# A two-layer graph network on one core: one fp32 product as three one-pass products, and row scales moved past the matmuls

## The reference

```python
def hypergraph_conv(x, adj, W, b):
    H = (adj != 0).astype(x.dtype)
    w = adj.reshape(N, -1)[:, :C]                  # the first row of adj
    xw = jnp.einsum('ncd,hd->nch', x, W)
    Dn = jnp.einsum('nce,ne->nc', H, w)            # 1/Dn where Dn > 0
    Be = H.sum(axis=1)                             # 1/Be where Be > 0
    m = Be[:, :, None] * jnp.einsum('nce,nch->neh', H, xw)
    out = Dn[:, :, None] * jnp.einsum('nce,neh->nch', H, m)
    return out + b
# layer 0
h = relu(hypergraph_conv(x, adj, W1, b1))          # 512 wide
h = layer_norm(h, gamma, beta)
y = hypergraph_conv(h, adj, W2, b2) + x            # 256 wide
x = _layernorm(x + y)
# layer 1
agg = einsum('bij,bjf->bif', adj, x) / maximum(adj.sum(-1), 1e-6)
x = _layernorm(x + relu(einsum('bnf,of->bno', concatenate([x, agg], 2), WL)))
```

## Time and profile before

| | |
|---|---|
| median of three runs | 1110.2 us (1109.57 to 1110.42) |
| profiled execution | 1110.66 us, span 1108.6 us |
| TensorE busy | 1093.2 us (99%), 6112 matmul records |
| VectorE busy | 699.6 us (63%) |
| ScalarE busy | 314.9 us (28%) |
| GpSimd busy | 182.5 us (16%) |

### The profile page before, as it was taken

How to read it: one execution, slowest core, us unless ns; L and a number is a source line. 1 busy time by engine, 2 the same in 40 slices (tenths; PEclk the granted TensorE clock), 3 DMA queues, 4 the chain that set the end, 5 groups by cost and what they waited for, 6 DMA issues and landing times.

```text
span 1108.6 us, 18544 instructions
## 1 busy us (share of the span) xinstructions
PE 1093.2 (99%) x6112; PEld 899.0 (81%) x6112; DVE 699.6 (63%) x1846; ACT 314.9 (28%) x705; POOL 182.5 (16%) x256
## 2 busy tenths in 40 slices
PE   7999999999999999999999999999999999999997
PEld 6879697796978969688796887969789697887966
DVE  4665595665955768548685486754766646856326
ACT  4342302422124221333113331143301433024220
POOL 0222004120031202211031110401104020041000
PEclk9999999999999999999999999999999999999999
DMA  7017612067211572124611445115442075300001
GB/s 280 20 39 153 150 41 58 0 151 152 55 40 31 120 151 57 38 65 101 146 47 38 96 102 121 41 38 129 103 89 71 4 151 115 65 9 1 1 1 39
DMA packets 64599, 86.18 MB, mean 78 GB/s; under 512 B 9024, under 2 KB 54720, under 8 KB 64576
## 3 DMA queue, kind: packets, MB, share of 16 engines
q1 hardware_dynamic: 63520, 85.88, 33.6%
q10 hardware_dynamic: 1056, 0.00, 0.1%
HBM read 77.47 MB, written 8.39 MB: 77 GB/s over the span
## 4 chain that ended last, share of the span: by engine, by line
PE 94%; DVE 4%; DMA 1%; ACT 0%; issue 0%; ACTq 0%; DVEq 0%
PE bank L731 40%; PE bank L802 10%; PE bank L840 10%; PE bank L862 10%; PE bank L824 10%; PE bank L759 10%; PE bank L832 3%; PE bank L848 1%; DVE adjT L539 1%; DMA small<-in_L_gnn_gamma_dram 1%; DVE HT L544 1%; PE bank L768 1%; DVE o_f L676 0%; DVE xres L680 0%; ACT m_hi L389 0%
## 5 line engine op out<-in xcount | busy, mean ns | idle before, releaser
L731 PE MATMUL bank<-yv,adjT 128*128 128x257 f32 x1024 | 223.3, 380 | 0.0
L731 PEld LDWEIGHTS bank<-yv,adjT 128*128 128x128 f32 x1024 | 194.1, 190 | 31.3 <-issue 3.8
L394 ACT ACTIVATE small<-mv,small 128x1 f32<-128x1 f32 x192 | 56.6, 295 | 362.6 <-DVE mv L521 266.9
L759 PE MATMUL bank<-x_hi,H 128*128 128x258 f32 x512 | 122.8, 289 | 0.8 <-DVE m_lo L526 0.8
L731 PE MATMUL bank<-x_hi,H 128*128 128x256 f32 x512 | 122.6, 283 | 0.0
L731 PE MATMUL bank<-m_hi,HT 128*128 128x256 f32 x512 | 121.6, 281 | 0.0
L731 PE MATMUL bank<-x_lo,H 128*128 128x256 f32 x512 | 121.1, 281 | 0.0
L731 PE MATMUL bank<-m_lo,HT 128*128 128x256 f32 x512 | 120.9, 280 | 0.0
L526 DVE SCALAR_TENSOR_TENSOR m_lo<-bank,small,m_hi 128x256 fp32r<-128x256 f32 x128 | 61.1, 483 | 94.2 <-ACT m_hi L389 94.1
L824 PE MATMUL bank<-W1T,zT 128*128 128x512 f32 x256 | 120.4, 593 | 0.0
L840 PE MATMUL bank<-gW2T,xnT 128*128 128x256 f32 x512 | 119.8, 380 | 0.0
(11 more groups left out here) (80 smaller groups left out, 1621.7 us busy)
## 6 DMA issues: line engine op xcount, KB each, us to landing
raw<-in_adj_dram SPq DMA_DIRECT2D x112, 256.0 KB, 8.5
adjB<-in_adj_dram SPq DMA_DIRECT2D x224, 128.0 KB, 3.4
x_in<-in_x_dram SPq DMA_DIRECT2D x28, 256.0 KB, 4.5
out_dram<-xres SPq DMA_DIRECT2D x112, 64.0 KB, 1.6
raw<-in_adj_dram SPq DMA_DIRECT2D x4, 1024.0 KB, 12.9
w_row<-in_adj_dram SPq DMA_DIRECT2D x8, 512.0 KB, 3.7
x_in<-in_x_dram SPq DMA_DIRECT2D x1, 1024.0 KB, 7.1
out_dram<-xres SPq DMA_DIRECT2D x4, 256.0 KB, 2.2
```

What stands on the lines that cost most here:

```text
L394: nc.scalar.activation(std[:, i:i + 1], mv[:, which, i, 1:2], ACT.Sqrt, bias=eps_c)\
L731: last = mm(bank(stage, i)[:, 0:n_cols], lhsT, rhs, start=(k == 0 and part == 0), stop=(k == NT - 1 and part == parts - 1))
L759: last = mm(*args, start=(c == 0 and n == 0), stop=(c == NT - 1 and n == 1))
```

## The change

P's operands are split in parts of 12 bits, `z` = z_high + z_low and W1 = W1_high + W1_low, whose products are exact in one pass. With high and low scaled copies the sum is made of three products: high x high and low x low go to P's bank, and the cross product of `z_high - 4096 z_low` and `W1_high - 4096 W1_low` to a bank of its own, **M**. The bias row of a tile becomes `hbias` = M x rDn_cross + b1: ScalarE reads M out of PSUM, GpSimd adds b1, and VectorE's hrow adds it to P x rDn_main. The names in the diff are W1_TURN and others for turns of the transpose banks, `SPLIT` = 4096, and `n_side` = 6 for the number of S1 tiles that run step by step.

W2 and WL have the mean of each row taken away once. Then Q of the relu'd row itself, scaled by `rstd_h` as it leaves PSUM, and V of `xres`, scaled by `rstd_1`, need no centring ahead of the transposes. `xres` is still normalised for the residual, now on ScalarE during L. The lags become 1 and 2, there are two slots of `hrow` in place of four, `xnT` lies where `w_row` does, and W2's preparation stands at the sixth step of the first S1.

```diff
-SECOND_CHUNK = {0: (0, 1, 2), 1: (3, 4), 2: (5, 6), 3: (7,)}
-LAG_T = 3
-LAG_Q = 4
-H_SLOTS = 4
+SECOND_CHUNK = {0: (0, 1, 2, 3, 4), 1: (5, 6, 7)}
+LAG_T = 1
+LAG_Q = 2
+H_SLOTS = 2
...
# SyncE
-            sp.dma_start(W2n[:, :, :], W2.rearrange("(t p) d -> p t d", p=P)).then_inc(W2_loaded, 16)
+            sp.dma_start(W1n[:, :, :], W1.rearrange("(t p) d -> p t d", p=P)).then_inc(W1_loaded, 16)
+            sp.dma_start(WLn[:, :, :], WL.rearrange("(t p) d -> p t d", p=P)).then_inc(WL_loaded, 16)
             sp.dma_start(x_in[:, :, :], x[0, :, :].rearrange("(t p) d -> p t d", p=P)).then_inc(x_loaded, 16)
             load_first_rows(0)
...
-                    sp.wait_ge(dn_ready, b * NT + NT)
-                    load_w(b + 1)
...
-                    load_graph(b + 1)
+                    load_raw(b + 1, 0)
+                    load_w(b + 1)
+                    for j in range(1, NT // 2):
+                        load_raw(b + 1, j)
...
# GpSimd
-            pool.wait_ge(rDn_ready, 1)
+            pool.wait_ge(rDn_ready, 2)
...
-                for i in range(NT):
-                    pool.wait_ge(q_hi_done, b * NT + i + 1)
-                    nc.gpsimd.tensor_tensor(x_lo[:, i, :], q_f32[:, i % 2, :], x_hi[:, i, 0:D].bitcast(F32),
-                                            ALU.subtract).then_inc(q_split, 1)
+                for s in range(NT + LAG_Q):
+                    if s < NT:
+                        pool.wait_ge(*emptied("M", s, b))
+                        nc.gpsimd.tensor_tensor(hbias[:, s % 2, :], hbias[:, s % 2, :], b1_row[:, :], ALU.add)\
+                          .then_inc(hbias_done, 1)
+                    if s >= LAG_Q:
+                        i = s - LAG_Q
+                        pool.wait_ge(q_hi_done, b * NT + i + 1)
+                        nc.gpsimd.tensor_tensor(x_lo[:, i, :], q_f32[:, i % 2, :], x_hi[:, i, 0:D].bitcast(F32),
+                                                ALU.subtract).then_inc(q_split, 1)
...
# ScalarE, first graph
-            for e in range(2, NT):
+            for e in range(2, TRANSPOSE_BANKS[0]):
                 take_m_hi("S1", e, 0, e)
+            take_weights(W2_TURN, [gW2T[:, 2 * k:2 * k + 2, :].rearrange("p k o -> p (k o)") for k in range(NH // 2)])
+            act.wait_ge(bank_full[TRANSPOSE_BANKS[0]], BW2_TURN + 1)
+            nc.scalar.activation(bW2_row[:, :], banks[TRANSPOSE_BANKS[0]][:, 0:D], ACT.Copy)\
+              .then_inc(bank_empty[TRANSPOSE_BANKS[0]], 1)
+            for e in range(TRANSPOSE_BANKS[0], NT):
+                take_m_hi("S1", e, 0, e)
...
# ScalarE, each graph
+                take_z_high(0)
+                act.wait_ge(rDn_ready, b * 2 + 2)
                 for s in range(NT + LAG_Q):
+                    if s == max(SECOND_CHUNK):
+                        take_z_high(1)
                     if s < NT:
-                        act.wait_ge(*emptied("P", s, b))
-                        nc.scalar.activation(hrow[:, s % H_SLOTS, :], hrow[:, s % H_SLOTS, :], ACT.Relu)\
-                          .then_inc(relu_done, 1)
-                    if s == max(SECOND_CHUNK) - 1:
-                        take_zT(1)
+                        act.wait_ge(*full("M", s, b))
+                        empties_bank(nc.scalar.activation(hbias[:, s % 2, :], bank("M", s)[:, :], ACT.Identity,
+                                                          scale=rDn_cross[:, s:s + 1]), "M", s)
                     if 0 <= s - LAG_T < NT:
                         i = s - LAG_T
                         act.wait_ge(*full("TH", i, b))
                         empties_bank(nc.scalar.activation(xnT[:, i % 2, :, :].rearrange("p k c -> p (k c)"),
                                                           bank("TH", i)[:, :], ACT.Copy), "TH", i)
                     if s < NT:
+                        act.wait_ge(*emptied("P", s, b))
+                        nc.scalar.activation(hrow[:, s % H_SLOTS, :], hrow[:, s % H_SLOTS, :], ACT.Relu)\
+                          .then_inc(relu_done, 1)
                         root("h", 0, std_h, s, b)
...
+                act.wait_ge(neg_mean_done, b + 1)
+                for i in range(NT):
+                    nc.scalar.activation(xres[:, i, :], xres[:, i, :], ACT.Identity, scale=rstd_1[:, i:i + 1],
+                                         bias=neg_mean_1[:, i:i + 1]).then_inc(normed["1"], 1)
...
# VectorE, each graph
+                take_z_low(0)
+                take_z_cross(0)
                 for s in range(NT + LAG_Q):
+                    if s == max(SECOND_CHUNK):
+                        take_z_low(1)
                     if s < NT:
                         dve.wait_ge(*full("P", s, b))
+                        dve.wait_ge(hbias_done, b * NT + s + 1)
                         empties_bank(nc.vector.scalar_tensor_tensor(
-                            out=hrow[:, s % H_SLOTS, :], in0=bank("P", s)[:, :], scalar=rDn[:, s:s + 1],
-                            in1=b1_row[:, :], op0=ALU.mult, op1=ALU.add), "P", s)
+                            out=hrow[:, s % H_SLOTS, :], in0=bank("P", s)[:, :], scalar=rDn_main[:, s:s + 1],
+                            in1=hbias[:, s % 2, :], op0=ALU.mult, op1=ALU.add), "P", s)
+                    if s == max(SECOND_CHUNK):
+                        take_z_cross(1)
                     if 0 <= s - 1 < NT:
                         inverse_root("h", std_h, rstd_h, s - 1, b)
-                        centre("h", 0, hrow[:, (s - 1) % H_SLOTS, :], rstd_h, s - 1, b)
...
-                        empties_bank(nc.vector.tensor_tensor(q_f32[:, i % 2, :], bank("Q", i)[:, 0:D],
-                                                             bW2_row[:, :], ALU.add), "Q", i)
+                        dve.wait_ge(rstd_done["h"], b * NT + i + 1)
+                        empties_bank(nc.vector.scalar_tensor_tensor(
+                            out=q_f32[:, i % 2, :], in0=bank("Q", i)[:, 0:D], scalar=rstd_h[:, i:i + 1],
+                            in1=bW2_row[:, :], op0=ALU.mult, op1=ALU.add), "Q", i)
...
# TensorE, each graph
+                        pe.wait_ge(*free("M", s, b))
+                        if s == 0:
+                            pe.wait_ge(W1_cross_done, ND)
+                        if s % (CH // P) == 0:
+                            pe.wait_ge(z_cross_done, b * (NCH * ND) + (s // (CH // P) + 1) * ND)
+                        nodes = slice(s * P, (s + 1) * P)
+                        for d in range(ND):
+                            last = mm(bank("M", s)[:, :], z_cross[:, d, nodes], W1_cross[:, d, :],
+                                      start=(d == 0), stop=(d == ND - 1))
+                        fills_bank(last, "M", s)
                         pe.wait_ge(*free("P", s, b))
                         for d in range(ND):
-                            last = mm(bank("P", s)[:, :], zT[:, d, s * P:(s + 1) * P], W1T[:, d, :],
-                                      start=(d == 0), stop=(d == ND - 1))
+                            mm(bank("P", s)[:, :], z_high[:, d, nodes], W1_high[:, d, :], start=(d == 0), stop=False)
+                            last = mm(bank("P", s)[:, :], z_low[:, d, nodes], W1_low[:, d, :],
+                                      start=False, stop=(d == ND - 1))
```

More of the change, by code:

```diff
@@ L92, in graph_net @@
         if s < NT:
+            add_job("M", s)
             add_job("P", s)
@@ L493, in sum_Dn @@
                     dve.wait_ge(dn_ready, b * NT + c)
-                nc.vector.scalar_tensor_tensor(out=unread[:, :], in0=raw[:, c, :], scalar=0.0, in1=w_row[:, :],
+                nc.vector.scalar_tensor_tensor(out=into[:, :], in0=raw[:, c, :], scalar=0.0, in1=w_row[:, :],
                                                op0=ALU.not_equal, op1=ALU.mult,
@@ L518, in moments @@
             def moments(norm, which, src, i, b):
-                nc.vector.bn_stats(stats[:, which, i, :], src)
+                nc.vector.bn_stats(stats[:, i, :], src)
                 dve.drain()
-                nc.vector.bn_aggr(mv[:, which, i, :], stats[:, which, i, :]).then_inc(var_done[norm], 1)
+                nc.vector.bn_aggr(mv[:, which, i, :], stats[:, i, :]).then_inc(var_done[norm], 1)
             def take_m_lo(stage, e, b, n):
@@ L555, in scale_W2T, with centre_weights @@
-            def scale_W2T():
-                for n in range(NH // 2):
-                    dve.wait_ge(bank_empty[TRANSPOSE_BANKS[n]], W2_TURN + 1)
-                    for k in (2 * n, 2 * n + 1):
-                        nc.vector.tensor_scalar(gW2T[:, k, :], W2T[:, k, :], gamma_c[:, k:k + 1], None, ALU.mult)\
-                          .then_inc(W2T_scaled, 1)
+            def centre_weights(parts, done):
+                for n, part in enumerate(parts):
+                    nc.vector.bn_stats(stats[:, n, :], part)
+                dve.drain()
+                for n, part in enumerate(parts):
+                    nc.vector.bn_aggr(mv[:, 0, n, :], stats[:, n, :])
+                dve.drain()
+                for n, part in enumerate(parts):
```

(23 more changed lines are left out.)

229 lines of the change are left out of this document (133 added, 96 removed), and 13 rows, old and new, of the table PRODUCT_BANKS.

## The result

The changed kernel takes 1236.3 us (median of four runs, 1235.1 to 1241.0) against 1109.9 us beside it (1109.2 to 1110.4): a ratio of 1.115 with a 95% interval of 1.112 to 1.118. The profiled execution has a span of 1234.0 us where the one before had 1108.6.

What follows compares the result with a forecast made beforehand. TensorE, busy 99%, bounds the kernel before; after the change a chain of handoffs at 5.50 us a tile does. 1110.66 + 107.2 for eight graphs + 16.4 for the first graph = 1234 us, stated range 1205 to 1280.

Steps and rivals of the forecast that it cites:

- TensorE, P 1.72 to 1.40: P on TensorE: four records become six one-pass products, 0.32 us less a tile, 20.5 us over 64 tiles if TensorE binds.
- The loop, 5.50 us a tile: P stage, relu to relu through moments, q, x_hi, x_lo, add and hrow: 5.50 us a tile against TensorE's 3.57.
- the ring: P stage's handoff chain: hbias(s+1) cannot start until root(s) and x_hi(s-2) are done on ScalarE, so tiles no longer overlap.
- The add, 1.35 between 1.15 and 1.79: GpSimd's 512-column add of b1, shown by no row: taken as 1.35 us, twice x_lo's price, with some start cost paid once.
- One graph, +13.4: From the end of S2's first half to the last Q: 52.0 us against 38.6, 107 us for eight graphs.
- hidden, with 0.6 to spare: Splitting z, some 4.1 us on ScalarE and VectorE, fits beside TensorE's five k-steps (4.7) before M(0); uncovered it costs 4.1.
- Centring and loads, 0: Centring moved into the weights costs nothing; w_row's later load counts 0, between 0 and 3 us a graph.
- rival 3: w_row late as well: VectorE's row sums wait in S3 and m_lo goes late, up to 3 us a graph, 1258; chance 0.07.
- The first graph, +16.4: First graph's setup: +6.3 for a later start and +10.1 for hbias(0)'s add behind GpSimd's residual passes, once, between 6 and 24.
- The sum: Whole kernel: 1110.66 + 107.2 + 16.4 = 1234 us; the main case alone 1212 to 1268.
- Rival 1: TensorE still binds, faster: ScalarE's copy of M runs a tile ahead and TensorE's 3.57 sets the pace, 1106.6; chance 0.05.
- Rival 2: TensorE falls to its lower clock in the gaps: 7.1 us a tile, some 10.6 us a graph more, 1319; chance 0.08.

Runs made afterwards that it cites:

- experiment 11: experiment 9 plus earlier first-graph setup, ScalarE scaling z_low behind relu(1) and doubling the first graph's x: 1104.8 us, ratio 0.9949 against the kernel before.
- experiments 1 to 3: Changed kernel with ScalarE's copy of M a tile ahead, with GpSimd's add ahead of x_lo, then with both: 1224.4, 1231.7 and 1134.2 us.
- 4: Changed kernel with GpSimd's add covering 256 of 512 columns, half of the bias left out: 1199.9 us.
- experiment 7: Changed kernel with VectorE making hbias in one pass from M's bank, without ScalarE's copy and GpSimd's add: 1130.5 us.
- experiment 5: Changed kernel with GpSimd's 16 first-graph residual passes waiting for the bias product instead of the row sums' end: 1234.6 us.
- experiment 3: Changed kernel with both orders changed: ScalarE's copy of M a tile ahead and GpSimd's add ahead of x_lo: 1134.2 us.
- experiment 9: experiment 7 with hbias(s+1) right behind hrow(s), M(s+1) behind P(s), and the second half's z_cross made by ScalarE and GpSimd: 1118.2 us.

## Why the prediction was right

It said 1234 (1205 to 1280) and slower with 0.94; 1236 was measured. The mechanism is the one that it named. That the total fits to 2 us is luck in part: a graph's 13.4 was 1.2 too long, eight times, and against it stood the first graph's 3.4, 1.5 in the second graph and 1.4 of low clock in each of four graphs, none of which is in the sum. By its steps:

- *TensorE, P 1.72 to 1.40.* Right: products 0.23 apart. TensorE would have gained, as experiment 11 shows.
- *The loop, 5.50 us a tile.* Right in its order, link by link, and a little too long: the last five steps have a mean of 5.36. relu to moments 0.66 (predicted 0.66), moments to q 0.87 (0.95), q to x_hi 0.52 (0.52), to x_lo 0.49 (0.49), to the add 0.60 (0.69), to hrow 1.33 (1.40), to relu 0.79 (0.79). What each run showed apart: experiments 1 to 3 that the two orders close the ring, 4 that the add lies on it, 7 that it is gone with the two handoffs.
- *The add, 1.35 between 1.15 and 1.79.* 1.284. The Trainium skill (GPSIMD Engine Reference, Elementwise, side-by-side), from which I had worked out an estimate of 1.25, was nearer here than my doubling of x_lo. The prediction's 0.717 for 256 columns was not "VectorE quiet": from 53.78 to 59.52 VectorE ran hrow, moments and a centring pass of 1.17 instead of 0.55 us. Beside an idle VectorE such a pass took 0.69 in the changed kernel. That page's advice to keep elementwise adds on VectorE (Engine selection) agrees with experiment 7's 741 ns for scale and add in one.
- *One graph, +13.4.* +12.2 from the fourth graph on; 15.2, 13.6 and 13.7 in the three ahead. In the later graphs relu(0) stands 8.2 after the end of S2's first half, as predicted. In the second graph it stood 9.7 after it since M(0) waited 1.16 us for z_cross, with relu(7) at 47.4 (47.2). So "hidden, with 0.6 to spare" failed there: VectorE came late to it.

```profile
219.44 1.29 DVE L688 TENSOR_TENSOR z_low<-bank,z_high 128x512 fp32r<-128x512 f32 x2 [4.60 <-issue]
```

VectorE's idle time there has no releaser. It stands at the first pass through the loop over graphs, and the later graphs don't have it; what it is the runs do not settle.

The other 1.4 us lie behind TH(7), which waits 3.05 us for relu(7) in every graph. In the first three graphs and the last the two Q's after it ran in part at the 1.2 GHz level, in the four between at full speed. The third and the fifth graph, TH(7) and the first product of S3, and the windows over them:

```profile
412.29 1.09 PE L939 MATMUL bank<-ident,hrow 128*128 128x128 f32 x4 [3.05 <-ACT hrow L489]
417.62 0.47 PE L829 MATMUL bank<-x_hi,H 128*128 128x256 f32 x1
...
707.28 0.63 PE L939 MATMUL bank<-ident,hrow 128*128 128x128 f32 x4 [3.05 <-ACT hrow L489]
711.25 0.47 PE L829 MATMUL bank<-x_hi,H 128*128 128x256 f32 x1
```

```profile
411.90:418.00 6.10, 5.71 (x22) 5.01 (x23) 1.89 (x5) 1.86 (x5) 1.34 (x2) 0.72 0.00 0
706.90:713.00 6.10, 5.72 (x34) 5.02 (x35) 2.37 (x6) 2.27 (x6) 1.71 (x3) 1.00 0.05 10
```

From TH(7) to S3 it is 5.33 us in the one and 3.97 in the other.

- *Centring and loads, 0.* Right: VectorE's waits for `w_row` are 1.1 us in all, and rival 3 is out.
- *The first graph, +16.4.* Too small by 3.5: relu(0) at 75.35 instead of 71.9. The residual passes began at 62.28 (59.3 predicted) and took 11.0 us instead of the 10.3 of the earlier trace rows; ahead of them TensorE had waited 3.0 us for H(7), 1.6 for the banks of W2's transposes and 2.8 for their copies. Their share as a cause was over-stated: experiment 5 won 2.7 of the 10.1, 4 at the most, since the row sums and z's split are next.
- *The sum.* The first relu came 3.4 late, all behind it took 102.8 us more than before where the sum had 104.4 (its 123.6 less the 19.2 up to that relu): 1.8 too little in all. The bounds beside it add up to 1211 and 1270, not 1212 and 1268.
- *Rival 1* was the nearest miss: with the order of experiment 3 it comes to 1134, not 1106.6, because a graph stayed at 134.5 us there and the first relu came 23.3 later than before. TensorE's own pace came only with experiment 9; which of its moves that needs I did not part.
- *Rival 2* is there, and costs little. Its 10.6 us a graph do not come out of its own prices (seven steps, each 1.64 longer, are 11.5). Its example, the products 0.21 us apart at 12.72, rests on their spacing, since the windows view has a granted clock of 1.00 there (12 to 14 us); in the changed kernel the same spacing (34.08 to 34.30) stands at 0.50. Windows of the changed kernel, of the first graph and of a later one (length, busy of five engines, granted clock, DMA share, GB/s):

```profile
82.00:88.00 6.00, 6.00 (x17) 4.93 (x18) 2.94 (x9) 1.99 (x4) 1.26 (x1) 0.51 0.00 0
...
520.00:572.00 52.00, 40.20 (x214) 33.32 (x213) 20.96 (x47) 20.96 (x44) 15.54 (x16) 0.97 0.12 29
```

A clock of 0.51 is the level of 1.2 GHz; it stands behind a wait of 3.83 us for the relu. The gaps of 1.4 to 1.7 us in each tile left 0.97, and from 231 to 260 us 1.00. So the Trainium skill's account of a resting level (TensorE: Matmul & The Clock Gate, What's actually happening) is borne out for the long gaps (4.40 and 3.83 us, and 3.05 us four times out of eight), and not as a price for each tile. In the tiles it cost little, since TensorE had slack: the first graph's steps (5.87, 5.16, 5.33, 5.25, 5.45, 5.29, 5.41) are nearly those of the others. Where TensorE had none, behind TH(7), it cost the 1.4 us of four graphs.

## What to carry to other kernels

When a result passes through one more engine, write the engines' lists side by side and follow one tile through them: a ring is closed by where an instruction stands in its list, not by how busy the engine is. Two engines that were at 28% and 16% came to hold this kernel back, and the same instructions in another order gave back 102 of 126 us. A pass that is added for the sake of a matmul should stand a tile ahead of its use on every engine that it crosses, and a setup that is paid once still has to be earned back.

## What the runs showed of the hardware

- VectorE's row sum and GpSimd's pass over 256 columns slow each other: 1.23 to 1.56 us and 0.69 to 1.19 us on the mean in experiment 5; in experiment 11, where nearly all of the eight passes stand beside sums, these took 12.07, 1.51 each. The Trainium skill (SBUF — State Buffer, Who interferes with whom) has a port pair that these two share as an exclusive lock. That they slow each other agrees. In experiment 11 a sum with its read-out came every 1.68 us (47.84 to 49.52), and in that time GpSimd did 1.1 passes; alone these take 1.34 and 0.77, in turn 2.1. So in these rows they overlap more than a strict lock would let them.
- GpSimd's add costs 0.737 us for 256 and 1.284 us for 512 columns, so some 0.19 us of it do not grow with the columns.
- Behind the same wait of 3.05 us at TH(7) TensorE's granted clock was 0.72 to 0.76 over the next 6 to 7 us in four graphs of the changed kernel, and 1.00 in the other four.
- After TensorE's wait of 4.40 us in the first graph, ten products stood 0.43 us apart at a granted clock of 0.51 (65.66 to 70.89), and then 0.23 (70.89 to 71.12) at 1.00:

```profile
65.66 1.22 PE L925 MATMUL bank<-W_cross,z_cross 128*128 128x512 f32 x2 [4.40 <-DVE z_cross L696]
66.68 0.63 PE L930 MATMUL bank<-W_high,z_high 128*128 128x512 f32 x1
67.10 0.63 PE L931 MATMUL bank<-W_low,z_low 128*128 128x512 f32 x1
```
